# A merged attention, feed-forward and router stage: a tile's second product one slot later, the batch sums one slot later

## The reference

```
x = x + L0_xattn(layernorm(x), ctx)      # an attention-free mixer, then norm, ReLU FFN 256-1024-256, norm
x = x + L0_ffn(layernorm(x))             # router: top 8 of 64 experts (256-64-256, SiLU) + 2 shared experts
x = x + L1_xattn(layernorm(x), ctx, ctx, mask)   # 16-head attention
x = x + L1_ffn(layernorm(x))             # binarised FFN 256-1024-256, GELU
```

## Time and profile before

| | us |
|---|---|
| median of 3 runs | 1244.63 |
| lowest and highest | 1239.29, 1244.81 |
| the profiled execution | 1242.67 |
| its span in the trace | 1240.9 |
| TensorE busy | 1140.9 (92%) |
| VectorE busy | 875.9 (71%) |
| ScalarE busy | 702.1 (57%) |
| mean granted TensorE clock | 0.981 of full speed |

### The profile page before, as it was taken

How to read it: one execution, slowest core, us unless ns; L and a number is a source line. 1 busy time by engine, 2 the same in 40 slices (tenths; PEclk the granted TensorE clock), 3 DMA queues, 4 the chain that set the end, 5 groups by cost and what they waited for, 6 DMA issues and landing times. The chain is left out here.

```text
span 1240.9 us, 19941 instructions
## 1 busy us (share of the span) xinstructions
PE 1140.9 (92%) x6928; PEld 991.6 (80%) x6928; DVE 875.9 (71%) x1656; ACT 702.1 (57%) x1066; POOL 343.1 (28%) x343
## 2 busy tenths in 40 slices
PE   4889898788779999999999989999999999989997
PEld 3677787677668999999999878778788788777887
DVE  5987758566755656656554444999989989997575
ACT  3223323655534444444443244988988988986755
POOL 1613111622421402403300054512522532333110
PEclk9989999898989999999999989999999999999999
DMA  9200000034324343343220032321421422310001
GB/s 320 68 1 1 1 1 1 1 100 105 64 66 144 98 143 108 104 137 107 97 94 11 1 100 78 112 74 53 133 74 43 143 92 87 97 40 5 15 33 41
DMA packets 68967, 92.88 MB, mean 75 GB/s; under 512 B 16016, under 2 KB 33168, under 8 KB 68752
## 3 DMA queue, kind: packets, MB, share of 16 engines
q1 hardware_dynamic: 67264, 89.67, 24.4%
q10 hardware_dynamic: 1616, 2.10, 0.5%
HBM read 80.45 MB, written 11.14 MB: 74 GB/s over the span
## 5 line engine op out<-in xcount | busy, mean ns | idle before, releaser
L2037 DVE CUSTOM_DVE_ANT_0 at_pr<-at_sc,at_mk 128x512 f32<-128x512 f32 x256 | 165.4, 683 | 25.5 <-PE at_sc L2268 24.9
L1941 ACT ACTIVATE at_pr<-at_pr,at_nmx 128x512 f32<-128x512 f32 x256 | 170.5, 717 | 17.6 <-DVE at_nmx L2037 16.9
L2179 DVE TENSOR_TENSOR W_1l<-at_pt,W_1h 128x1024 fp32r<-128x1024 f32 x128 | 155.8, 1217 | 5.9 <-ACT W_1h L1936 5.4
L1936 ACT ACTIVATE W_1h<-at_pt 128x1024 fp32r<-128x1024 f32 x128 | 130.8, 1022 | 32.4 <-PE at_o L2302 30.4
L2283 PE MATMUL at_pt<-ident,at_pr 128*128 128x128 f32 x1024 | 134.6, 274 | 14.8 <-DVE W_1l L2179 14.1
L2283 PEld LDWEIGHTS at_pt<-ident,at_pr 128*128 128x128 f32 x1024 | 114.5, 141 | 38.2 <-issue 17.3
L228 ACT ACTIVATE moe_hs<-moe_hid,cols 128x512 f32<-128x512 f32 x120 | 82.8, 690 | 103.8 <-PE moe_hid L114 102.7
L247 DVE TENSOR_TENSOR moe_hl<-moe_ms,moe_hh 128x512 fp32r<-128x512 f32 x104 | 80.4, 773 | 64.2 <-ACT moe_hh L220 64.2
L261 DVE TENSOR_TENSOR moe_ms<-moe_hs,gate 128x512 f32<-128x512 f32 x104 | 78.7, 757 | 60.3 <-ACT moe_hs L228 59.7
L220 ACT ACTIVATE moe_hh<-moe_ms 128x512 fp32r<-128x512 f32 x104 | 65.8, 632 | 94.1 <-DVE moe_ms L261 94.1
L654 ACT ACTIVATE f_hs<-f_hid,cols 128x512 f32<-128x512 f32 x56 | 38.5, 687 | 136.3 <-PE f_hid L114 114.3
(11 more groups left out here) (304 smaller groups left out, 3294.4 us busy)
## 6 DMA issues: line engine op xcount, KB each, us to landing
gate<-expert_weights SPq DMA_DIRECT2D x256, 128.0 KB, 3.0
w_stage<-in_ew SPq DMA_DIRECT2D x32, 256.0 KB, 4.0
at_kp<-at_heads SPq DMA_DIRECT2D x96, 64.0 KB, 2.7
at_qp<-at_heads SPq DMA_DIRECT2D x96, 64.0 KB, 2.7
w_stage<-in_mask SPq DMA_DIRECT2D x16, 256.0 KB, 4.1
at_rb<-at_recip SPq DMA_DIRECT2D x64, 64.0 KB, 2.0
w_stage<-in_w SPq DMA_DIRECT2D x8, 256.0 KB, 8.0
w_stage<-in_sw SPq DMA_DIRECT2D x8, 256.0 KB, 3.3
```

The source lines that it names most:

```text
L1936: act.activation(PH[0][:, n % 2, :], PT[n % 2][:, :, :].rearrange("p c q -> p (c q)"), ACT.Copy)\
L1941: act.activation(pr_of(t)[:, x, :], pr_of(t)[:, x, :], ACT.Exp, bias=nmx[:, t % 4, x:x + 1], scale=-1.0).then_inc(s["ex"], 1)
L2037: dve.tensor_tensor_reduce(pr_of(t)[:, x, :], SB[x][:, :], mk[u // 2 % 2][:, j, :], -float(HD) ** -0.5, 3.0e38, ALU.add, ALU.min, nmx[:, t ...
L2179: dve.tensor_tensor(PH[1][:, n % 2, :], PT[n % 2][:, :, :].rearrange("p c q -> p (c q)"), f(PH[0][:, n % 2, :]), ALU.subtract).then_inc(s[ ...
```

## The change

In every slot TensorE's `output` is now that of the tile three slots back, not two. The loop over slots runs one slot longer at the end on TensorE and on VectorE, so that the last three outputs and the last sum are done. The batch sums move on VectorE from slot 2 to slot 3. ScalarE, GpSimd and SP are unchanged.

```
# vector engine
-                for t in range(SLOTS if i < B + EARLY else 3):
+                for t in range(SLOTS if i < B + EARLY else 4):
...
-                    if t == 2 and 1 <= i <= B:
+                    if t == 3 and 1 <= i <= B:
                         add_y(i - 1)
-                    if t == 2 and i > B:
+                    if t == 3 and i > B:
                         add_expert_y(i - B - 1)
# tensor engine
-                for t in range(SLOTS if i < B + EARLY else 2):
+                for t in range(SLOTS if i < B + EARLY else 3):
...
-                    if 2 <= n < LAST + 2:
-                        output(n - 2)
+                    if 3 <= n < LAST + 3:
+                        output(n - 3)
```

## The result

| | before | after |
|---|---|---|
| median, us (runs) | 1243.47 (20) | 1247.2 (20) |
| lowest and highest | 1237.32, 1246.14 | 1242.25, 1252.11 |
| the profiled execution | 1242.67 | 1251.06 |
| its span | 1240.9 | 1249.2 |
| its mean granted clock | 0.981 | 0.976 |

The ratio is 1.0032, with a 95% interval of 1.0018 to 1.0045: the changed kernel is slower, by about 4 us, and clearly so, although by less than the 0.5% of the forecast. Forecast was no change (-0.3 us). The profiled execution is one of the slower ones, 3.9 us above its median, so differences of the two traces overstate the loss.

The account below looks back on a forecast made before the run. The prediction took a gate-to-gate latency ring through VectorE and ScalarE to bound the expert iterations, not TensorE's output waits. 1242.67 + 0 + 2.4 - 2.7 + 0 = 1242.4, plus 1.96 for the median: 1244.3 us, range 1238.5 to 1249.

Parts of the forecast that it names:

- the sum: Whole kernel: 1242.67 + 0 + 2.4 - 2.7 + 0 = 1242.4, with the median 1.96 above the profiled execution: 1244.3 us.
- the second rival: TensorE's clock falls behind merged and new waits; five more falls on the path cost 7.5 us: 1252; chance 0.06.
- the ring: Expert iterations: gate-to-gate latency loop through VectorE, ScalarE, router's weights and SP's store and load; only shortening it counts as gain.
- Sums where the mixer runs: Iterations 1 and 2: each sum enters VectorE's gapless work before `make_y`, +1.2 us each, +2.4 together; bounds 0 and +5.8.
- the chain: Mixer work without slack behind the sum: `make_y`, ScalarE's split and exponentials, TensorE's `value`; delayed 1.2 us in iteration 1.
- Sums where the experts run: Iterations 4 to 6: sum leaves the gate-to-gate path for VectorE idle time, -0.9 us each, -2.7 in all; bounds 0 and -6.3.
- Waits on `low`: First stage: TensorE's ten output waits, 14.5 us, go, but later waits replace them; 0 gained, bounds 0 and all 14.5.
- The full refund: First rival: ten waits go with nothing in their place, plus slow clock behind them, 19 us: 1225; chance 0.05.
- Start 0, tail 0: Freed 1.7 us at the start gains nothing; the extra output at the end hides under SP's gate loads, 1.8 us cover.
- The third rival: Expert iterations gain nothing and the mixer's delay stays: 1244.63 + 2.4 = 1247.0, or 1248.7 with the tail uncovered; chance 0.25.

Follow-up runs that it names:

- second profile: The changed kernel run once more, unedited, beside the kernel before on the same chip; ratio to before 1.0028 (1.0012 to 1.0044).
- FFN-only kernel: Against the kernel before: output lag of three slots and late sums for tiles 0 to 31 alone, expert tiles as before; ratio 1.0023 (1.0009 to 1.0038).
- experts-only one: Against the kernel before: output lag of three slots and late sums from tile 32 on, first four sums as before; ratio 1.0020 (1.0004 to 1.0035).
- sums between the reciprocals: The changed kernel with the sums of batches 0 and 1 put between slot 2's two reciprocals, not in slot 3; ratio to before 1.0013 (0.9996 to 1.0031).
- without two sums: The changed kernel without the VectorE sums of batches 0 and 1, that part of the result left out; ratio to before 1.0000 (0.9980 to 1.0020).
- with the wait filled: The changed kernel with 13 extra 128x512 products before iteration 2's first output, where TensorE waits 3.18 us; ratio to before 1.0012 (0.9997 to 1.0027).

## Why the prediction was wrong

Two steps failed, both in what **the sum** is added up from. It has no term for the clock: the clock stood as the second rival, with five falls needed and 0.06. And the gain of the experts' sums, -2.7, was too large by about 2 us. The reason given against the clock, "after such a fall TensorE mostly has slack until the ring's next step, so that the loss is absorbed", is what the traces contradict. With `turn_weights` in its old place, from VectorE's last step on the router's weights (L902) to ScalarE's copy of them (L743), which is on the ring, took 3.9 to 4.1 us where the clock held and 4.6 to 5.7 us where a fall stood at `turn_weights`: 5.3 in the changed kernel (290.15 to 295.49), 5.5 in its second profile (322.10 to 327.58), and 4.7 in the kernel before (284.60 to 289.26). So a fall there isn't absorbed, and the kernel before shows it too.

- **The clock, how much.** Within the 20 runs of the changed kernel 0.001 of granted clock goes with 1.06 us. Its 32 runs have a mean of 0.9785, the 90 of before 0.9820: 0.0035, so some 3.7 us, of a difference of the means of 4.4 (1246.5 and 1242.0). What is left, 0.7, is what the forecast's terms were to give (-0.3). The same working leaves +2.0 for the FFN-only kernel and -1.1 for the experts-only one, where the forecast's terms are +2.4 and -2.7. As an estimate, 0.0035 of 1247 us is 8.7 us more at half the clock in each execution, about two more falls of the lengths seen here, not five. This is a correlation and an estimate: a longer wait also lowers the mean clock without costing anything by that, and the slopes of the kernels lie between 0.4 and 1.1. That the clock costs time on the path is shown in the profiles; how much of the mean loss is its, isn't.
- **Sums where the mixer runs, +2.4.** Right, where the clock holds (93.3 against 90.9, in two profiles each). The FFN-only kernel, +2.9 at a nearly unchanged clock, agrees. The wait of 3.18 us for the second sum brought a fall on top in three of the four profiles that have it, worth 0.9 to 2.2 us. The prediction counted new waits of that kind as standing beside other work; the work behind this one was on the chain.
- **Sums where the experts run, -2.7.** The sign is right, the size isn't. From the gate to the weights iteration 5 took 21.9 us in all five profiles that have the changed code there (303.76 to 325.65 in the first), 22.4 in the kernel before (297.21 to 319.65), and 22.1 in the FFN-only kernel (302.92 to 325.06), which has the old code in this iteration and no clock fall before 323.6. So the sum's move is worth 0.2 to 0.3 us in an iteration with the clock held, 0.5 against the one profile of before, and not 0.9. The prediction read slot 2's gate at 303.68, 6.5 us behind the first gate, with its 0.39 of waiting for an activation, as the ordinary case. That stands in a clock fall of the kernel before (299.7 to 303.7); in the FFN-only kernel it is 6.0. In the changed kernel it is 5.7, with a wait of its own:

```profile
303.76 0.69 DVE L838 TENSOR_TENSOR f_hs<-f_hs,gate 128x512 f32<-128x512 f32 x1 [7.36 <-DMA gate<-expert_weights]
...
309.47 0.69 DVE L838 TENSOR_TENSOR f_hs<-f_hs,gate 128x512 f32<-128x512 f32 x1 [0.81 <-ACT f_hs L654]
...
325.65 0.43 DVE L902 TENSOR_TENSOR rt_cwx<-rt_ex,rt_cwx 128x256 fp32r<-128x256 f32 x1
```

Over the three iterations together, from the first `turn_weights` to the last, the changed code took 105.1 and 103.5 us in its two profiles and 102.1, 101.4 and 101.2 in the runs with the sums between the reciprocals, without two sums and with the wait filled. The kernel before took 104.7, and the FFN-only kernel, with one output more there, 103.0. The three shortest and the last have a mean clock of 0.98, the others 0.95. So one profile against another can show anything from +0.4 to -3.5 here, and the shorter ones are those with the higher clock.
- **Waits on `low`, 0.** Right: all 14.5 us went and as much and more came back in front of L902, L872 and the sums. The full refund was 22 us off.
- **Start 0, tail 0.** Right in the compared profiles. `turn_weights` of the last router batch to the next stage took 13.7 us before (356.61 to 370.30) and 13.8 after (363.14 to 376.89); in the changed kernel's second profile, with a fall at that `turn_weights`, 15.2. SP's gate loads end about 2.2 us before the next stage, as they did (374.7 and 376.89, before 368.1 and 370.30).
- **The third rival**, no gain in the ring and the mixer's delay, 1247.0, is the number that came out. Its mechanism is near what the traces show with the clock held, a small gain in the ring and +2.4; but the loss in the means is 4.4, not 2.4. That the number fits is luck: it starts from a median of 3 runs, 1244.63, and that of 20 was 1243.47.

The time (1247.2) lay inside the range and the change was under 0.5%; the small but clear loss was missed. The rule of the Trainium skill that I weighed there ("TensorE: Matmul & The Clock Gate", "HAM oscillation — how this bites in real kernels") has waits put following tiles on half the clock, and the traces do show that here, at 202.59 and 307.60, at the granted 0.50.

## What to carry to other kernels

When several short waits of the matrix engine merge in longer ones, price the clock behind each by what stands right after it: a fall costs little in front of idle time and about half its own length in front of a step of the chain (5.5 us at the lower level cost 2.6 here). And look for such falls in the profile of the kernel before, ahead of taking a term from a row that stands in one. Moving a small vector operation by a slot can take it from idle time into a gapless piece; the rows show which. And where a stage is a ring of latency, look for the work that stands in the ring without belonging there: moving one hidden tile from ahead of `turn_weights` gained 0.4%, and taking away all of the outputs' waits for f_hl gained nothing.

## What the runs showed that I had not expected

The same wait in the same place sometimes lowers the clock and sometimes doesn't. The wait of 3.04 to 3.05 us before the transposes at 134 us stands in every kernel. It left the granted clock at 1.00 in the stretch from 134 to 140 us before and in the changed kernel. In the second profile of the changed kernel, the same program, the stretch had 0.72, and in the experts-only kernel it was

```profile
134.00:140.00 6.00, 5.99 (x34) 5.78 (x35) 3.71 (x7) 2.28 (x4) 0.00 (x0) 0.72 0.00 0
```

The wait of 3.18 us for the second sum was followed by a fall in three profiles and by none in a fourth. Waits of 1.82 to 2.15 us were at times followed by one. So one profile can be 2 us off from the next in a stage for the clock alone, and only means over many runs, with the granted clock beside them, tell such kernels apart. And adding 13 useless products, 2.9 us of work, did not make the kernel slower but, as far as the intervals tell, some 2 us faster.
